# Agents' stage: the low parts of the expert weights in 24 GpSimd instructions in place of six

## The reference, cut to what matters

```
def _L1_attn_ref(x, w_qkv, w_conv1):          # x: 8 x 1024 in the signature, 8 x 288 x 256 here
    agent = q @ w_conv1                       # one number per row
    agent_attn = softmax(sum over rows of (agent * scale) * k)      # 8 x 256
    agent_v = softmax(agent_attn . v)         # 8 x 288
    agent_v = sum over rows of agent_v * v    # 8 x 256
    return softmax(agent[:, :, None]) * agent_v[:, None, :]

def _L1_ffn_ref(x, gate_w, W1, W2, Ws1, Ws2):
    scores = softmax(x @ gate_w.T); top 2 of 8 experts
    h = x @ W1.T        # per expert 256 -> 2*192; the shared expert Ws1: 256 -> 2*384
    y, g = halves of h; out = (y * silu(g)) @ W2.T
```

## Time and profile before

| | |
|---|---|
| median of 3 runs | 664.82 us (660.91, 664.82, 666.14) |
| the profiled execution's own time | 661.77 us |
| its span, first to last instruction | 660.0 us |
| mean granted TensorE clock | 0.937 of full speed |
| busy: PE, DVE, ACT, POOL | 85%, 64%, 41%, 33% |
| agents' stage | 405.95 to 444.85 us |

### The profile page before, as it was taken

One profiled execution on the slowest core, in us unless ns is written; L12 is line 12 of the kernel. 1 busy time (PEld: TensorE's weight loads), 2 busy tenths in 40 slices (PEclk: granted clock), 3 DMA queues, 4 the chain that ended last, 5 costly groups with the idle time before them and its releaser, 6 DMA issues. The chain is left out here.

```text
span 660.0 us, 11552 instructions
## 1 busy us (share of the span) xinstructions
PE 562.3 (85%) x4020; PEld 468.7 (71%) x4020; DVE 423.0 (64%) x1047; ACT 269.5 (41%) x561; POOL 214.9 (33%) x299
## 2 busy tenths in 40 slices
PE   5899758999999999999999776455998899999982
PEld 4799647687878778787868463224787799997772
DVE  2598966668777777778768765658579332223166
ACT  1533345353636454554636235102411355554410
POOL 2467760411111101111111115703101677777500
PEclk9999969899999999999999978556999999999998
DMA  7222203000000000000000242202200233333276
GB/s 227 75 65 64 60 6 96 2 1 1 1 1 1 2 1 1 1 1 1 1 2 1 71 169 72 49 0 73 73 0 1 85 105 99 105 105 100 92 226 205
DMA packets 27443, 37.02 MB, mean 56 GB/s; under 512 B 4541, under 2 KB 22782, under 8 KB 27390
## 3 DMA queue, kind: packets, MB, share of 16 engines
q1 hardware_dynamic: 23166, 24.78, 12.3%
q0 software_dynamic: 4224, 11.54, 5.6%
HBM read 25.95 MB, written 10.35 MB: 55 GB/s over the span
## 5 line engine op out<-in xcount | busy, mean ns | idle before, releaser
L664 PE MATMUL ps<-b_x_hi,wa_hi 128*128 128x288 f32 x192 | 58.8, 306 | 6.0 <-DVE w1raw L1366 4.4
L1589 POOL TENSOR_TENSOR c_rstd<-c_ve,mhalf 128x2 f32<-128x2 f32 (+2 forms) x20 | 13.4, 671 | 151.2 <-DVE c_ve L563 151.2
L2517 DVE TENSOR_TENSOR w1raw<-ps,w1raw 128x192 f32<-128x192 f32 x43 | 15.4, 358 | 68.5 <-ACT w1raw L2318 68.5
L665 PE MATMUL ps<-b_x_lo,wa_hi 128*128 128x288 f32 x192 | 57.2, 298 | 0.0
L666 PE MATMUL ps<-b_x_hi,wa_lo 128*128 128x288 f32 x192 | 57.1, 297 | 0.0
L2577 POOL DMA_INDIRECT kv<-x_rows,r_src_i x43 | 41.7, 970 | 25.8 <-DVE r_src_i L2439 11.1
L1635 POOL TENSOR_TENSOR w1raw<-w1raw 128x288 f32<-128x288 f32 x16 | 16.1, 1026 | 96.9 <-DVE w1raw L1366 96.9
L1227 ACT CAST b_y_hi<-b_yt 128x256 fp32r<-128x256 f32 x32 | 12.9, 402 | 81.8 <-DVE b_yt L1348 81.6
L2204 PE MATMUL ps<-w,w1raw 96*128 x172 | 44.6, 381 | 1.2 <-ACT w1raw L2330 1.2
L1360 DVE TENSOR_TENSOR w1raw<-ps,decay 128x1024 f32<-128x1024 f32 x32 | 38.5, 1221 | 8.3 <-PE ps L1026 8.3
L664 PEld LDWEIGHTS ps<-b_x_hi,wa_hi 128*128 128x128 f32 x192 | 36.6, 191 | 9.0 <-DVE w1raw L1366 6.0
(11 more groups left out here) (383 smaller groups left out, 1603.4 us busy)
## 6 DMA issues: line engine op xcount, KB each, us to landing
d_x_hi<-y_rows SPq DMA_DIRECT2D x18, 256.0 KB, 3.9
w1raw<-in_W_t SPq DMA_DIRECT2D x8, 384.0 KB, 5.0
x_rows<-w1raw SPq DMA_DIRECT2D x6, 384.0 KB, 2.5
a_xt<-in_x_t SPq DMA_DIRECT2D x8, 256.0 KB, 3.7
a_xfl<-in_x_flat SPq DMA_DIRECT2D x8, 256.0 KB, 2.7
out<-hres SPq DMA_DIRECT2D x16, 128.0 KB, 3.7
w<-in_W_t SPq DMA_DIRECT2D x8, 192.0 KB, 4.1
w1raw<-in_Ws_t SPq DMA_DIRECT2D x1, 768.0 KB, 8.5
```

The lines of the kernel that those rows point to most:

```text
L664: nc.tensor.matmul(out, x_hi, w_hi, start=start, stop=False)
L665: nc.tensor.matmul(out, x_hi, w_lo, start=False, stop=False)
```

## The change

In place of one subtraction for each of the six parts, GpSimd issues four, each of a quarter of the part's columns: 160 columns of both halves, 2 x 160 = 320 numbers in a partition. All 7680 numbers of a partition are computed as before, in the same order of columns. The six waits for `w_rounded` stay as they are, ahead of each four. Nothing else in the program differs; the order of instructions on every other engine is the same.

```diff
+        def piece_of(w, b, n):
+
+            m = NJ * 2 * HE // NGR // 4
+            first = (4 * b + n) * m
+            return w[:, :, first:first + m]
...
             for b in range(NGR):
                 pool.wait_ge(w_rounded, b + 1)
-                nc.gpsimd.tensor_tensor(part_of(g["w1_lo"], b), part_of(g["w1raw"], b),
-                                        part_of(g["w1_hi"], b).bitcast(F32), ALU.subtract)
+                for n in range(4):
+                    nc.gpsimd.tensor_tensor(piece_of(g["w1_lo"], b, n), piece_of(g["w1raw"], b, n),
+                                            piece_of(g["w1_hi"], b, n).bitcast(F32), ALU.subtract)
```

## The result

The changed kernel takes 667.99 us (median of 11 runs, 666.37 to 669.81) against 663.15 us before (11 runs, 660.87 to 666.73): a ratio of 1.0062, 95% interval 1.0039 to 1.0086, so 0.6% slower; the two medians lie 4.8 us apart. The forecast was 661.8 us. The profiled execution took 667.58 us, its span 665.8 us against 660.0.

A forecast was written before the change was run, and what follows sets the result against it. The agents' stage was taken as bound by one dependent chain, with two VectorE instructions on it blocked by POOL's subtractions. Shorter blocks gain 1.5 us: 663.3 - 1.5 = 661.8 us, range 658.5 to 666.0.

The forecast's parts named there:

- What bounds the stage: Agents' stage: one dependent chain sets its length; VectorE lines 1842, 1854 and 1861 wait for POOL's running subtraction.
- upper bound of 2.47 us: Summed gain at lines 1854 and 1861 if both run free; 1861 then starts at 422.49 and ends at 422.66.
- The pieces: POOL's 24 subtractions: 0.87 us each, one every 0.82, ending at 427.7 instead of 425.1; the later end costs nothing.
- The block at line 1842: VectorE, now 0.70 us, then at most until a piece ends; worth nothing, since VectorE next idles for PE.
- The block at line 1854: VectorE, 128x16, on the chain: let in at the running piece's end, 421.18 instead of 422.31, gaining 1.13 us.
- lower bound of the gain, 0.84 us: Line 1854 with a whole piece ahead of it, 0.90 us instead of 1.74.
- Line 1861: VectorE, 8x8, on the chain: ends at a piece's end, 423.64 instead of 425.13, making the summed gain 1.49 us.
- Rival B: VectorE is not let in between pieces until POOL is done at 427.7; 4.5 us slower, 667.8 us; chance 0.04.
- Lines 1863 and 1867: VectorE, one input in SBUF, one in PSUM, newly beside POOL: undisturbed, costing nothing; if wrong, up to 0.87 us each.
- The clock: Granted clock, back at about 457 us: nothing added if its rise moves with the work, otherwise up to 0.65 us lost.
- rival A: The clock's rise keeps its place in time: gain 0.85 us, time 662.4 us; chance 0.15.

The follow-up runs named there:

- e1: Kernel before (six subtractions) plus six VectorE probe subtractions with both inputs in SBUF, off every path; one run, 665.21 us.
- e9: Kernel before (six subtractions), with the last two held back until VectorE has made e_diag; 660.90 us (12 runs), ratio 0.9967.
- e2: Changed kernel (24 pieces) plus six VectorE probe subtractions with both inputs in SBUF; one run, 663.81 us.
- e3: Changed kernel, but groups 0 to 3 as one subtraction each and only groups 4 and 5 in four pieces each; 661.47 us, ratio 0.9975.
- e8: Changed kernel, with GpSimd waiting ahead of group 4 until its own 16th piece is complete; 661.38 us.
- e11: Changed kernel, with each piece waiting until the one before it is complete; 661.93 us.
- e12: Changed kernel, with the long-fulfilled wait for w_rounded ahead of every piece instead of every fourth; 668.60 us.
- e4: Changed kernel, but only groups 0 to 3 in four pieces each and groups 4 and 5 as one subtraction each; 667.38 us, ratio 1.0050.
- e13: Changed kernel plus a single VectorE probe subtraction (agr minus agr) ahead of row sum 5; 665.65 us.
- e14: Changed kernel plus a single VectorE probe subtraction (agr minus agr) ahead of row sum 8; 662.86 us.
- e7: Changed kernel plus a single VectorE probe subtraction (agr minus agr) ahead of row sum 14; 672.96 us.

## Why the prediction was wrong, step by step

- **What bounds the stage, and that three VectorE instructions wait for the running subtraction**: right. e1 shows it with five more instances, and e9 shows what the two on the path are worth. The upper bound of 2.47 us was too high by 0.37, since it took the mask product's 1.57 whole, where PE's own transposes leave 1.25 of it, and 0.17 for a free `e_diag`, which takes 0.22: the chain can gain 2.10. That e9's time fell by 2.2 is in part luck, since what the clock gave in the stage (1.73) and took in the mixture (1.96) happened to cancel.
- **The pieces**: right. 0.87 us forecast, 0.855 the median; every 0.82; the end at 427.95 (forecast 427.7); POOL then idle for 21.99 us, and nobody waited for it.
- **The block at line 1842**: right, 0.31 us and hidden.
- **The block at line 1854**: this is the step that failed. That "the instruction ends at 421.18 in place of 422.31" rested on VectorE being let in at the end of the piece that runs. It ended at 427.99: 5.41 us lost in place of 1.13 gained. The lower bound of the gain, 0.84 us "with a whole piece ahead of it", was no bound.
- **Line 1861**: its gain came for another reason: 0.85 us, since the burst was over.
- **Rival B** was the mechanism: "VectorE is not let in between pieces", priced at 4.5 us slower. The two places gave 5.41 - 0.85 = 4.56. That its time, 667.8, is so near the measured 667.99 is in part luck: the clock gave 1.87 us back in the stage and took 2.84 in the mixture, of which B had neither. I gave it 0.04, on two handovers in the trace. Both of them were between long subtractions, of which no more than three had run since VectorE's last access; they said little about the sixteenth short one, twelve pieces after the last access. Its reason, that pieces overlap by 0.04 us and so a queued one can take hold first, is not enough either: the pieces of e2 overlap as much, and every end of them at which VectorE waited let it in.
- **Lines 1863 and 1867**: not tried by the changed kernel, in which the burst was over. In e3 they ran beside the pieces and kept their length.
- **The clock**: the sum let the low stretch move with the work, rival A let it keep its place, at 0.65 us. e9 is as A says: its mixture starts 3.88 us earlier and the clock rises at 457 us as before, which cost 1.44 us. In the changed kernel the mixture starts 2.96 us later and the rise comes 7 us later, at 464. Neither the high clock within the stage nor the second low stretch at 515 us stood in the prediction; with them the clock took 2.84 - 1.87 = 0.97 us of the 5.80.

What stays open is what wears out. The Trainium skill, GPSIMD Engine Reference, section Instruction dispatch, says that consecutive GpSimd instructions are no barrier between its eight cores: each goes on to the next instruction when its own share is done. If the cores drift apart by some piece, there may be no moment at which none of them holds the port. That a wait for completion opens it (e8, e11), that a fulfilled wait does not (e12), and that e4's long subtractions behind short ones stay shut all agree with it; no run here shows the cores, and a backlog of issued instructions would explain the same runs. Nor is it found why 5 pieces were too many in e13 and not in e2, and 6 not in e13 and e14.

## What to carry to other kernels

An instruction cut into short ones on GpSimd is not a finer interleaving with VectorE: a burst of them can shut a two-input VectorE instruction out until its end. Where a short VectorE instruction on the critical path lasts as long as GpSimd is busy, and GpSimd has slack, hold GpSimd's work back behind a semaphore of that instruction, or break the burst with a wait for its own completion. A break of that kind was tried before VectorE asked (e8, e11), not as a rescue of one that is already shut out. And two handovers seen between long instructions are no evidence for the sixteenth between short ones: ask what the trace has not shown yet, and give that rival its weight.

## What the runs showed of the hardware

- A VectorE instruction with two inputs in SBUF, or a multiplication of such an input by a scalar (`e_diag`), started 0.06 to 0.65 us into a GpSimd subtraction of 0.86 us, ended 0.02 to 0.04 us after the end of that subtraction, or, once the burst had gone on for 9 to 12 of them without such an access (in e13 for 5), 0.03 to 0.04 us after the end of the last of 24 (7.15 us, and 9.67 us in e7). Long subtractions behind them did not open it (e4). The Trainium skill, SBUF — State Buffer, section Who interferes with whom, says that the engine which issues first gets the shared ports for its whole instruction and blocks the other (so put for VectorE's two-port modes), and that issue order decides who blocks; here VectorE was blocked for up to twelve instructions of the other (e7), most of which started after it.
- The row sums of line 1850, with one input in SBUF and one in PSUM, kept their 0.41 to 0.42 us in every kernel.
- With the same work and the same length of stage to within a few us, the granted clock in the stage differed: 0.50 from 410 us on before, 0.93 in a window of 8 us in the changed kernel, 0.71 in one in e9.
